# A layer norm's last pass moved from VectorE to ScalarE in the down projection of a quantised feed-forward

## The reference

```python
def _layernorm(x, axis=-1, eps=1e-05):
    m = jnp.mean(x, axis=axis, keepdims=True)
    v = jnp.var(x, axis=axis, keepdims=True)
    return (x - m) / jnp.sqrt(v + eps)
...
xq = _act_fake_quant(x, clip_x[0])
gate = jnp.einsum('bsh,ih->bsi', xq, _weight_fake_quant(w_gate))
up = jnp.einsum('bsh,ih->bsi', xq, _weight_fake_quant(w_up))
h = _act_fake_quant(jax.nn.silu(gate) * up, clip_down[0])
return jnp.einsum('bsi,hi->bsh', h, _weight_fake_quant(w_down))
...
x = _layernorm(x + _L0_ffn_ref(x, ...), axis=-1)
```

## Time and profile before

| | |
|---|---|
| median of three runs | 3324.82 us (3321.77 to 3327.7) |
| profiled execution, its own time | 3335.67 us |
| its span, first to last instruction | 3333.9 us |
| TensorE matmul, busy | 2692.8 us, 81% |
| VectorE, busy | 2510.2 us, 75% |
| ScalarE, busy | 1182.5 us, 35% |
| GpSimd, busy | 620.9 us, 19% |
| mean granted TensorE clock | 0.894 |

### The profile page before, as it was taken

The page is one execution under the profiler, slowest core; times in us unless marked ns, Lnnn a source line. Parts: engine busy times, 40 slices in busy tenths (PEclk is TensorE's granted clock), DMA queues, the critical chain, the costliest instruction groups (busy, mean ns, idle before and its releaser), DMA issues. The chain is left out here.

```text
span 3333.9 us, 88364 instructions
## 1 busy us (share of the span) xinstructions
PE 2692.8 (81%) x35334; PEld 1912.9 (57%) x35356; DVE 2510.2 (75%) x4464; ACT 1182.5 (35%) x2016; POOL 620.9 (19%) x800
## 2 busy tenths in 40 slices
PE   7577777777777755999999995697769999968987
PEld 5455655555555543677777763344456767646664
DVE  6888887888888872477777783887857787834887
ACT  5233333333333320122222221654446565521221
POOL 3232222333322221000000000002600000002343
PEclk9789888888888866999999997899989999988888
DMA  3000000010000101301111112545941212142231
GB/s 88 3 15 28 29 28 29 28 29 28 29 28 29 47 22 64 128 20 51 51 50 50 50 48 89 196 176 179 319 116 51 76 50 76 59 143 83 83 94 51
DMA packets 229643, 234.68 MB, mean 70 GB/s; under 512 B 24112, under 2 KB 157872, under 8 KB 229296
## 3 DMA queue, kind: packets, MB, share of 16 engines
q1 hardware_dynamic: 229296, 229.70, 21.6%
HBM read 136.84 MB, written 92.81 MB: 69 GB/s over the span
## 5 line engine op out<-in xcount | busy, mean ns | idle before, releaser
L1132 PE MATMUL ctxatt_banks<-ctxatt_xT,ctxatt_wq 128*128 128x256 f32 x1024 | 232.9, 381 | 2.9 <-ACT ctxatt_qT L1208 2.1
L1171 PE MATMUL ctxatt_banks<-ctxatt_wo,ctxatt_oT 128*128 128x512 f32 x512 | 230.8, 604 | 4.9 <-DVE ctxatt_norm_y L1277 4.9
L826 DVE TENSOR_TENSOR delta_a<-delta_t_sys 128x30 f32<-128x30 f32 (+14 forms) x480 | 223.3, 465 | 10.3
L849 DVE SCALAR_TENSOR_TENSOR delta_conv<-delta_line,delta_conv_w,delta_conv 128x256 f32<-128x256 f32 x384 | 206.9, 560 | 3.4 <-DVE delta_ss L772 2.1
L829 DVE TENSOR_TENSOR delta_t_sys<-delta_t_sys,delta_a 128x30 f32<-128x30 f32 (+14 forms) x480 | 200.2, 417 | 11.4
L1132 PEld LDWEIGHTS ctxatt_banks<-ctxatt_xT,ctxatt_wq 128*128 128x128 f32 x1024 | 190.0, 191 | 28.7 <-ACT ctxatt_qT L1208 3.3
L393 POOL TENSOR_TENSOR delta_conv<-delta_conv,delta_product 128x256 f32<-128x256 f32 x192 | 148.7, 784 | 263.0 <-ACT delta_product L658 262.7
L508 PE MATMUL delta_banks<-delta_states,delta_kqT 32*32 32x32 f32 x4096 | 60.3, 209 | 154.0 <-DVE delta_states L868 95.2
L489 PE MATMUL delta_banks<-delta_xT,delta_wkT 128*128 128x256 f32 x512 | 135.9, 416 | 43.3 <-ACT delta_beta_T L640 35.8
L656 ACT ACTIVATE delta_conv<-delta_line,delta_conv_b,delta_conv_w 128x256 f32<-128x256 f32 x192 | 115.3, 601 | 153.3 <-POOL delta_conv L393 141.6
L1171 PEld LDWEIGHTS ctxatt_banks<-ctxatt_wo,ctxatt_oT 128*128 128x128 f32 x512 | 96.4, 193 | 117.0 <-issue 110.5
(11 more groups left out here) (328 smaller groups left out, 6728.3 us busy)
## 6 DMA issues: line engine op xcount, KB each, us to landing
h<-ffn_hid SPq DMA_DIRECT2D x66, 256.0 KB, 2.0
ffn_hid<-h SPq DMA_DIRECT2D x6, 1536.0 KB, 13.0
wkv_xT<-xT SPq DMA_DIRECT2D x64, 129.0 KB, 2.8
delta_xT<-xT SPq DMA_DIRECT2D x64, 128.0 KB, 3.0
delta_x<-x SPq DMA_DIRECT2D x16, 512.0 KB, 3.6
xT<-delta_newT SPq DMA_DIRECT2D x64, 128.0 KB, 2.8
x<-delta_new SPq DMA_DIRECT2D x16, 512.0 KB, 3.5
ctxatt_xT<-xT SPq DMA_DIRECT2D x64, 128.0 KB, 2.6
```

The lines of the kernel that those rows point to most:

```text
L826: c.did(dve.tensor_tensor(terms, t_sys[:, j + 1:, j:j + 1].to_broadcast([P, rows, j]), t_sys[:, j:j + 1, 0:j].to_broadcast([P, rows, j]), ...
L849: c.did(dve.scalar_tensor_tensor(to, line[:, i, g, :, j:j + P], conv_w[:, i, g, j:j + 1], to, ALU.mult, ALU.add))
L1132: mm = pe.matmul(b_q[:, i * B * P:(i + 1) * B * P], wq[:, k, pair * P:(pair + 1) * P], xT_sb[:, n.parity, k], start=k == 0, stop=k == KB - 1)
L1171: mm = pe.matmul(b_o[:], oT[:, b, k, :], wo[:, k, :], start=k == 0, stop=k == PAIRS - 1)
```

## The change

VectorE's `finish` of tile n-2 is taken out of its step. ScalarE gets a `finish` of its own, which stands at the head of its step, ahead of the quantising passes of tile n. It computes the same value as y * rstd + shift, with shift = -mean * rstd. GpSimd's `root` therefore has four operations instead of two: after `var_eps` and `rstd` it multiplies mean by rstd and subtracts the product from a tile of zeros (`nought`). ScalarE waits for the fourth. Four waits change with it: `weigh` of row r waits for ScalarE's finish of the same row of the tile before (as `norm.y` has one buffer); TensorE's transposes wait for `finished` row by row rather than for all four rows; SP's store of `new` waits for `finished`; and GpSimd's `root` waits until the tile before is finished. The class `ScaledNorm` moves up in the file, so that every line behind it has a number 28 to 30 higher.

```diff
+class ScaledNorm(Norm):
...
+        self.OPS = self.SUMMED + 2 * rows
+        self.ROOT_OPS = 4
+
+    def root(self, pool, n, eps, exponent, zero):
+        wait(pool, self.done, n, self.OPS, self.MOMENTS)
+        wait(pool, self.finished, n, self.rows, 0)
+        mean = self.moments[:, :, 0]
+        pool.tensor_tensor(self.var_eps[:], self.moments[:, :, 1], eps[:, 0:self.rows], ALU.add).then_inc(self.rooted, 1)
+        wait(pool, self.rooted, n, self.ROOT_OPS, 1)
+        pool.tensor_tensor(self.rstd[:], self.var_eps[:], exponent[:, 0:self.rows], ALU.pow).then_inc(self.rooted, 1)
+        wait(pool, self.rooted, n, self.ROOT_OPS, 2)
+        pool.tensor_tensor(self.shift[:], mean, self.rstd[:], ALU.mult).then_inc(self.rooted, 1)
+        wait(pool, self.rooted, n, self.ROOT_OPS, 3)
+        pool.tensor_tensor(self.shift[:], zero[:, 0:self.rows], self.shift[:], ALU.subtract).then_inc(self.rooted, 1)
+
+    def finish(self, act, n, r, target):
+        wait(act, self.rooted, n, self.ROOT_OPS, self.ROOT_OPS)
+        act.activation(target, self.y[:, r], ACT.Identity, bias=self.shift[:, r:r + 1], scale=self.rstd[:, r:r + 1]).then_inc(self.finished, 1)
...
-            norm = Norm(m2, "norm", FROWS, added)
+            norm = ScaledNorm(m2, "norm", FROWS, added)
...
                     def weigh(n, r):
                         wait(dve, multiplied, n, FROWS, r + 1)
-                        if r == 0:
-                            wait(dve, norm.done, n, norm.OPS, 0)
+                        wait(dve, norm.finished, n, FROWS, r + 1 - FROWS)
...
                         if n:
                             scale_h(n, 0)
-                        if t2 := n.back(2):
-                            finish(t2)
                         if t:
                             weigh(t, 0)
...
                 def _(act):
+                    def finish(n):
+                        wait(act, newT_made, n, FROWS, -FROWS)
+                        gone(act, new_stored, n, 16 * B)
+                        for r in range(FROWS):
+                            norm.finish(act, n, r, new[:, n.parity, r])
+
                     def step(n):
+                        if t := n.back(2):
+                            finish(t)
                         if n:
                             wait(act, multiplied, n, FROWS, -FROWS)
...
-                            wait(pe, norm.done, t, norm.OPS, norm.OPS)
                             for r in range(FROWS):
+                                wait(pe, norm.finished, t, FROWS, r + 1)
                                 wait(pe, newT_kept, t, FROWS, r + 1 - FROWS)
```

More of the change, by code:

```diff
@@ L191, in root, with __init__ @@
         pool.tensor_tensor(self.rstd[:], self.var_eps[:], exponent[:, 0:self.rows], ALU.pow).then_inc(self.rooted, 1)
+class ScaledNorm(Norm):
+    def __init__(self, m, name, rows, summed=None):
+        super().__init__(m, name, rows, summed)
+        self.shift = m.sbuf(f"{name}_shift", [P, rows])
+        self.finished = m.sem(f"{name}_finished")
+        self.OPS = self.SUMMED + 2 * rows
[14 more added lines that the diff above has]
+        act.activation(target, self.y[:, r], ACT.Identity, bias=self.shift[:, r:r + 1], scale=self.rstd[:, r:r + 1]).then_inc(self.finished, 1)
 DH = 16
@@ L1676, in quantised_feed_forward @@
             added = sem2("added")
-            norm = Norm(m2, "norm", FROWS, added)
+            norm = ScaledNorm(m2, "norm", FROWS, added)
+            nought = sb2("nought", [P, FROWS])
             h_here = [[sem2(f"h_here{i}_{j}") for i in range(2)] for j in range(2)]
@@ L1715, in step @@
                         if t := n.back(3):
-                            wait(sp, norm.done, t, norm.OPS, norm.OPS)
+                            wait(sp, norm.finished, t, FROWS, FROWS)
                             sp.sem_inc(passed, 1)
@@ L1734, in _ @@
                     pool.memset(zero[:], 0.0).then_inc(zeroed, 1)
+                    pool.memset(nought[:], 0.0)
                     def add(n):
@@ L1744, in step @@
                             add(t)
-                            norm.root(pool, t, eps, half)
+                            norm.root(pool, t, eps, half, nought)
                     pipelined(pool, FSTEPS, 3, step)
@@ L1771, in moments @@
                         norm.take_moments(dve, c, n)
[L1773 to L1778, removed]
                     def step(n):
@@ L1839, in _ @@
                     pipelined(pe, FSTEPS, 3, step)
[L1843 to L1867, removed]
 WT = P
```

## The result

The change took 3338.8 us, the median of 7 runs (3334.91 to 3346.6), against 3324.82 us of before (7 runs, 3315.86 to 3328.62). The medians lie 14.0 us apart, where 15.1 were forecast. The ratio worked out from all the runs is 1.0051, with a 95% interval of 1.0035 to 1.0067; that is 17 us, from 12 to 22, so that both numbers lie within it.

The account below looks back on a forecast made before the run. The stage was taken to run at VectorE's pace before and at the chain through ScalarE's queue after. Steps 12.6, last matmuls' clock 0.85 and stage end 1.6 sum to 15.1 us: 3339.9 us from 3324.82, range 3330 to 3348.

Parts of the forecast that it names:

- The chain: One step, from one tile's aggregates to the next, through GpSimd's root and ScalarE's finish and passes: 16.19 us against 14.11.
- Five steps: Whole steps having both a finish and a quantising: 5 x 2.08 = 10.4 us more.
- The sixth: From tile 5's aggregates to tile 7's clip: 12.81 us against 10.61, 2.2 us more.
- The end: Stage's end: 0.85 us, half of 1.69, for the last matmuls' lower clock; 1.6 us for longer root and finishing rows.
- The bound of 0.4 us for a clip with less of an addition beside it: Lower bound: second clip faster if GpSimd's additions have run already as a third, 2.4 us less in all.
- The upper bound: ScalarE waiting for a store of x once or twice at 3.9 us, or dearer finishing rows: +20 us.
- VectorE's relief: Rival: VectorE's busy time falls 1.92 us a step and decides, 11.5 us faster, 3313 us; chance 0.05.
- DMA sets the step: Rival: full DMA rings hide the new waits, only the stage's end costs 1.6 to 2.5 us, 3327 us; chance 0.09.
- TensorE's clock: Rival: with longer gaps TensorE stays at 1.2 GHz and bounds the step, 52 us more, 3376 us; chance 0.03.
- ScalarE's copies: Rival: their waits for stores delay the finish behind them, three steps at 4 us more each, 3352 us; chance 0.06.
- what the profile would show: Profile after: steps of 16.2 us, VectorE idle about 2.2 us before the first clip, DMA share below 1.
- The rule of the Trainium skill: Where VectorE is saturated, moving work to ScalarE may pay; by it the time would be 3313 us.

Follow-up runs that it names:

- interleaved: The change with ScalarE's order made finishing rows 0 and 1, first quantising pass, rows 2 and 3, second pass; steps 15.51 to 15.70 us, stage 149.13 us, one run.
- two_buffers_no_h: two_buffers without the loads of h from tile 2 on, so the stage's values differ; stage 127.06 us, one run.
- two_buffers: The change with a second buffer for norm.y and ScalarE doing both quantising passes, then the finish, then the copies; stage 143.80 us, ratio 1.0016.

## Why the prediction was right

*The chain.* It had every term: 16.19 us forecast, 15.95 to 16.14 us measured. Term by term in the step shown: aggregates to shift 3.42 (forecast 3.42); four rows and the two passes, from 2329.24 to 2337.23, 7.99 (8.02); to the clip 0.04 (0.03); clip to weigh 1.19 (1.19); to the statistics 0.60 (0.60); statistics 2.38 (2.48); aggregates 0.41. The 0.10 us of the statistics are GpSimd's last addition: before, it ended at 2338.61, and the fourth row's statistics had to wait for it; after, it ended at 2340.48, before their turn came.

*Five steps* came to 80.28 us (ends of the aggregates of tiles 0 and 5, 2309.69 and 2389.97) against 70.74: 9.5 us, forecast 10.4, 5 x 16.19 us against 5 x 14.11. Measured were 16.06 and 14.15 us a step. *The sixth* took 12.75 us from there to the end of the last clip, forecast 12.81. *The start*, which I hadn't counted, was 0.7 us shorter, with more of the first matmuls at the higher clock (20.24 instead of 20.90 us for 86).

*The end.* I took half of 1.69 us for the clock at the last group of matmuls, and it took 11.52 us against 9.44, 2.1 us more. From the clip to the last aggregates it was 15.4 us instead of 13.9: 1.5 us, forecast 0.85. From there to the x store it was 5.06 instead of 3.52 us: 1.5, forecast 1.6. The sum of the parts, -0.66 + 9.54 + 2.14 + 1.47 + 1.54, is 14.0 us, that of the stage. The mechanism is the forecast one, but that the total came within 1.1 us is in part luck: half of 1.69 us was a guess and 0.6 us too low for its stretch, the steps were 0.9 us too high, and the start was left out.

*The bound of 0.4 us for a clip with less of an addition beside it* didn't come true in the change (1.27 us in the step shown, as before), but did in interleaved (0.85). The upper bound was added up too low: one or two waits of 3.9 us on top of 15.1 + 0.85 give 20 to 24 us, not 20.

*The rivals.* VectorE's relief was real, 2.5 us of busy time less a step (1.92 us of it the four rows, 0.48 a first clip of 0.96 us instead of 1.44), and worth nothing while ScalarE stood in the way; two_buffers_no_h shows what it is worth with both ScalarE and DMA out of it, steps of 11.8 to 13.1 us. There TensorE is at work for 15.76 and 15.94 of 16 us in the windows shown, more than VectorE, and VectorE waits for it 13 times, 13.3 us in all; TensorE is then the likely limit, which no run tests. That DMA sets the step is refuted for before and after by the two runs without loads, though its share was what I had read, and it is the next limit behind VectorE: the gain of 2 us a step in two_buffers was lost to it. TensorE's clock was low at the beginning of four of the last six groups (10.68 to 12.20 us instead of 9.44) and back at 2.4 GHz within each; in the last one the granted clock is 0.50 from 2403.1 to 2407.3 us and 1.00 from 2407.4 on. The length of the gap ahead doesn't tell which: before the change, groups behind gaps of 3.13 and 3.35 us took 9.44 us, though the prediction read the 11.13 us behind 2.89 us as the gap's doing; after the change, one behind 5.45 us took 10.68 and one behind 3.53 us 11.13. ScalarE's copies never waited for a store after the change.

*Wrong in what the profile would show:* the DMA share is 0.93 in the step from 2325 to 2341 us, but in the three behind it 1.05 to 1.07, not below 1. A share near 1 doesn't say that anyone waits.

The rule of the Trainium skill that was weighed (page "Perfetto Trace Analysis", section "Optimizing Scalar/DVE Operations") names VectorE's load as the condition. Here VectorE had the load, and with it lightened the step was 2 us longer, so the trace of the change doesn't agree. With the same work moved, in another order and with a second buffer, the first steps of two_buffers were 1.0 to 2.6 us shorter than those of the kernel before, as long as DMA allowed it.

## What to carry to other kernels

Before moving work to an idle engine, look at what stands behind it in that engine's queue and who waits for that. ScalarE was idle half the time, but its second pass ended 0.03 us before VectorE needed it, and most of its idle time in a step (4.56 us) lay ahead of the moved work's inputs. If the work must go there, put the operations that others wait for first, and give the moved work a buffer of its own so that nobody waits for it; then ask what the next limit is, and check by leaving its work out. Here that limit was DMA: it took back what the steps had won, and the lead that was left came from the end of the stage.

## What the runs showed of the hardware

Some of VectorE's and GpSimd's operations on SBUF hold one another up. The same addition of four numbers a partition (L209) took 0.20 us on its own (2418.20) and 1.68 us when it started 0.17 us behind VectorE's scaling (2325.70 and 2325.87), ending just behind it; the clip of 3072 columns took 0.96 us alone and 1.96 us when it started during one of GpSimd's additions (2334.01 in interleaved), and the clips of 2560 columns ended 0.69 us after the addition beside them in both kernels. The Trainium skill, page "SBUF — State Buffer", section "SBUF: two separate sides", says that the two share a pair of ports, which the operation that starts first holds to its end, where VectorE's operation is in a mode that uses two ports or reads two inputs from SBUF. The trace agrees for these operations, with those numbers; which mode they ran in, no trace here shows. It decided the 0.4 us between interleaved and its forecast.
